# Sums over d in a three-layer interaction network: from Vector-engine reductions to ScalarE's accumulator

## The reference, cut to what matters

```python
B, M, D = 512, 32, 64            # SIZES = (128, 128, 128)
h = x0
for i in range(3):
    Wk = Ws[i].reshape(128, h.shape[1], M)
    xk = relu(einsum('bhd,bmd,ohm->bod', h, x0, Wk) + bs[i][None, :, None])
    if i != 2:
        outs.append(xk[:, :64]); h = xk[:, 64:]
    else:
        outs.append(xk)
return concatenate([o.sum(axis=-1) for o in outs], axis=1)     # (512, 256)
```

## Time and profile before

| | |
|---|---|
| median of 3 runs | 1762.95 us (1762.19 to 1766.04) |
| the profiled execution | 1765.33 us |
| its span, first to last instruction | 1763.5 us |
| mean granted TensorE clock | 0.993 |
| TensorE, Vector engine, ScalarE, GpSimd busy | 99%, 95%, 74%, 96% of the span |

### The profile page before, as it was taken

One profiled execution on the slowest core, in us unless ns is written; L12 is line 12 of the kernel. 1 busy time (PEld: TensorE's weight loads), 2 busy tenths in 40 slices (PEclk: granted clock), 3 DMA queues, 4 the chain that ended last, 5 costly groups with the idle time before them and its releaser, 6 DMA issues.

```text
span 1763.5 us, 19227 instructions
## 1 busy us (share of the span) xinstructions
PE 1742.0 (99%) x6740; PEld 1270.2 (72%) x6740; DVE 1676.0 (95%) x915; ACT 1307.9 (74%) x1218; POOL 1694.4 (96%) x451
## 2 busy tenths in 40 slices
PE   7899999999999999999999999999999999999998
PEld 4577777777777777777777777777777777777776
DVE  5999999999999999999999999999999999999996
ACT  3777777777777777777777777777777777777774
POOL 2799999999999999999999999999999999999996
PEclk8999999999999999999999999999999999999999
DMA  6424324334333243243243343332332432433410
GB/s 241 134 81 143 122 93 143 106 110 137 93 129 135 88 136 135 81 143 124 92 142 112 105 139 97 123 135 88 136 135 81 143 128 87 144 111 105 140 31 21
DMA packets 53600, 205.87 MB, mean 117 GB/s; under 512 B 10624, under 2 KB 11776, under 8 KB 45056
## 3 DMA queue, kind: packets, MB, share of 16 engines
q1 hardware_dynamic: 52992, 203.86, 35.0%
q10 hardware_dynamic: 512, 0.79, 0.2%
HBM read 153.75 MB, written 0.52 MB: 87 GB/s over the span
## 4 chain that ended last, share of the span: by engine, by line
PE 95%; DMA 2%; DVE 1%; ACT 1%; issue 0%; SPq 0%; POOL 0%; ACTq 0%; DVEq 0%; POOLq 0%
PE ACC L535 26%; PE ACC L526 26%; PE ACC L528 25%; PE ACC L519 15%; PE ACC L541 3%; DMA X<-in_xrows 1%; DMA H<-H 1%; DVE ZS L287 1%; DVE ZL L303 0%; POOL ZL L383 0%; ACT ZH L426 0%; ACT H L443 0%; ACT HP L409 0%; DVE S L317 0%; SPq L194 0%
## 5 line engine op out<-in xcount | busy, mean ns | idle before, releaser
L383 POOL TENSOR_TENSOR ZL<-ZS,ZH 128x2048 fp32r<-128x2048 f32 (+1 forms) x446 | 1693.7, 3846 | 60.9 <-ACT ZH L426 59.5
L287 DVE TENSOR_TENSOR ZS<-HP,X 128x2048 f32<-128x2048 f32 x448 | 1012.3, 2283 | 61.4 <-issue 46.4
L426 ACT ACTIVATE ZH<-ZS 128x2048 fp32r<-128x2048 f32 (+1 forms) x446 | 706.3, 1597 | 17.4 <-DVE ZS L287 15.5
L526 PE MATMUL ACC<-ZH,WL 128*128 128x512 f32 x1728 | 540.5, 427 | 5.1 <-DVE WL L261 4.2
L535 PE MATMUL ACC<-ZL,WH 128*128 128x512 f32 x1728 | 487.9, 396 | 7.0 <-DVE ZL L303 3.6
L528 PE MATMUL ACC<-ZH,WH 128*128 128x512 f32 x1728 | 486.7, 396 | 0.0
L409 ACT ACTIVATE HP<-H 128x512 f32<-128x512 f32 x256 | 152.8, 597 | 374.0 <-DVE ZS L287 361.9
L526 PEld LDWEIGHTS ACC<-ZH,WL 128*128 128x128 f32 x1728 | 326.0, 189 | 123.4 <-issue 51.6
L528 PEld LDWEIGHTS ACC<-ZH,WH 128*128 128x128 f32 x1728 | 325.1, 188 | 92.0 <-issue 15.3
L535 PEld LDWEIGHTS ACC<-ZL,WH 128*128 128x128 f32 x1728 | 324.4, 188 | 88.2 <-DVE ZL L303 5.2
L278 DVE TENSOR_TENSOR ZP<-HP,X 128x2048 f32<-128x2048 f32 x128 | 293.2, 2290 | 5.4 <-ACT HP L409 5.4
(11 more groups left out here) (34 smaller groups left out, 396.8 us busy)
## 6 DMA issues: line engine op xcount, KB each, us to landing
X<-in_xrows SPq DMA_DIRECT2D x62, 2048.0 KB, 7.6
H<-H SPq DMA_DIRECT2D x252, 128.0 KB, 2.3
XD<-in_xdup SPq DMA_DIRECT2D x64, 256.0 KB, 2.9
H<-H SPq DMA_DIRECT2D x252, 64.0 KB, 2.0
X<-in_xrows SPq DMA_DIRECT2D x4, 1024.0 KB, 7.9
X<-in_w SPq DMA_DIRECT2D x1, 896.0 KB, 10.5
X<-in_w SPq DMA_DIRECT2D x1, 832.0 KB, 14.8
H<-H ACTq DMA_DIRECT2D x4, 128.0 KB, 7.2
```

Source lines behind the costliest of these rows:

```text
L287: nc.vector.tensor_tensor(ZS[:, m % PSLOTS, :, :], h, x, ALU.mult).then_inc(product_ready, 1)
L383: nc.gpsimd.tensor_tensor(ZL[:, n % LSLOTS, c, :], ZS[:, m % PSLOTS, c, :], ZH[:, n % HSLOTS, c, :], ALU.subtract).then_inc(low_by_pool, 1)
L426: nc.scalar.activation(ZH[:, n % HSLOTS, c, :], src, ACT.Copy).then_inc(high_ready, 1)
L526: nc.tensor.matmul(acc, wl[:, k, :], ZH[:, n % HSLOTS, c, :], start=(first and k == 0), stop=False)
```

## The change

ScalarE's relu that fed a sum is cut into eight pieces of 64 columns, one for each sample of the tile. Each piece writes back into the accumulation bank that it reads and hands the sum of its outputs, one number per row, straight to its column of S12 or S3 (`accum_out`). `R12`, `R3`, the Vector engine's `sum12` and `sum3` and their semaphores are gone; a zeroed tile `BLANK` takes R3's place for the warm-up matmuls. The relus of the hidden rows (L443) are as they were. The last transposes wait for relu_done in place of the sums, and the last one also for out12_ready.

```diff
--- before.py
+++ after.py
@@ -118,8 +118,7 @@
         ZS = sb("ZS", [128, PSLOTS, G, T])
         ZH = sb("ZH", [128, HSLOTS, G, T], f32r)
         ZL = sb("ZL", [128, LSLOTS, G, T], f32r)
-        R12 = sb("R12", [128, T])
-        R3 = sb("R3", [128, T])
+        BLANK = sb("BLANK", [128, T])
         S12 = sb("S12", [128, B + BT])
         S3 = sb("S3", [128, B])
 
@@ -154,7 +153,6 @@
         low_by_pool, low_by_dve, low_used = sem("low_by_pool"), sem("low_by_dve"), sem("low_used")
         hidden_done = [sem("hidden_done2"), sem("hidden_done3")]
         relu_done = [sem(f"relu_done{n}") for n in range(3)]
-        sums12, sums3 = sem("sums12"), sem("sums3")
         tr_done, tr12_done = sem("tr_done"), sem("tr12_done")
         outs_ready, out12_ready, stored = sem("outs_ready"), sem("out12_ready"), sem("stored")
 
@@ -303,20 +301,6 @@
                 nc.vector.tensor_tensor(ZL[:, n % LSLOTS, :, :], ZP[:, :, :], ZH[:, n % HSLOTS, :, :],
                                         ALU.subtract).then_inc(low_by_dve, 1)
 
-            def sum12(i):
-                lo, hi = (0 if live(i) else HID), (2 * HID if live(i - 1) else HID)
-                if live(i):
-                    dve.wait_ge(relu_done[0], i + 1)
-                if live(i - 1):
-                    dve.wait_ge(relu_done[1], i)
-                nc.vector.reduce_sum(S12[lo:hi, BT * i:BT * i + BT],
-                                     R12[lo:hi, :].rearrange("p (b d) -> p b d", d=D), AX.X).then_inc(sums12, 1)
-
-            def sum3(t):
-                dve.wait_ge(relu_done[2], t + 1)
-                nc.vector.reduce_sum(S3[:, BT * t:BT * t + BT],
-                                     R3[:, :].rearrange("p (b d) -> p b d", d=D), AX.X).then_inc(sums3, 1)
-
             def gather12(n):
                 if n < BLOCKS - 1:
                     dve.wait_ge(tr_done, n + 1)
@@ -350,8 +334,6 @@
                     if i == 1:
                         low(i, 1, 0)
                     product(i, 1, 2)
-                if 0 <= i - 1 <= TILES:
-                    sum12(i - 1)
                 if live(i - 1):
                     if i > 1:
                         low(i, 1, 0)
@@ -360,20 +342,17 @@
                     product(i, 2, 0)
                     product(i, 2, 1)
                     product(i, 2, 2)
-                    if live(i - 3):
-                        sum3(i - 3)
                     low(i, 2, 0)
                     product(i, 2, 3)
             for n in range(BLOCKS - 1):
                 gather12(n)
                 gather3(n)
             gather12(BLOCKS - 1)
-            sum3(TILES - 1)
             gather3(BLOCKS - 1)
 
         @block.gpsimd
         def _(pool):
-            nc.gpsimd.memset(R3[:, :], 0.0).then_inc(blank, 1)
+            nc.gpsimd.memset(BLANK[:, :], 0.0).then_inc(blank, 1)
             for g in POOL_NO:
                 n, m = SPLIT_NO[g], SLOT_NO[g]
                 if n >= LSLOTS:
@@ -425,6 +404,14 @@
                     src = ZS[:, SLOT_NO[g] % PSLOTS, c, :]
                 nc.scalar.activation(ZH[:, n % HSLOTS, c, :], src, ACT.Copy).then_inc(high_ready, 1)
 
+            def relu_sums(acc, rows, b, to, t, done):
+
+                for n in range(BT):
+                    d = slice(D * n, D * n + D)
+                    last = nc.scalar.activation(acc[rows, d], acc[rows, d], ACT.Relu, bias=b[rows, :],
+                                                accum_out=to[rows, BT * t + n:BT * t + n + 1])
+                last.then_inc(done, 1)
+
             def relu(t, layer):
                 acc = ACC[LAYER_NO[t + layer, layer] % BANKS]
                 if layer == 0 and t < HEADS:
@@ -433,9 +420,7 @@
                     act.wait_ge(low_used, SPLIT_NO[t + layer, layer, Q - 1 if layer else 0] + 1)
                 b = bias_sb[:, layer:layer + 1]
                 if layer == 2:
-                    if t >= 1:
-                        act.wait_ge(sums3, t)
-                    nc.scalar.activation(R3[:, :], acc[:, :], ACT.Relu, bias=b).then_inc(relu_done[2], 1)
+                    relu_sums(acc, slice(0, 2 * HID), b, S3, t, relu_done[2])
                     return
                 hid, rest = (slice(HID, 2 * HID), slice(0, HID))[::1 if layer == 0 else -1]
                 if t >= 1:
@@ -444,10 +429,7 @@
                                      bias=b[hid, :]).then_inc(hidden_done[layer], 1)
                 if spread_by_act(t):
                     spread_hidden(act, t, layer)
-                if t + layer >= 1:
-                    act.wait_ge(sums12, t + layer)
-                nc.scalar.activation(R12[rest, :], acc[rest, :], ACT.Relu,
-                                     bias=b[rest, :]).then_inc(relu_done[layer], 1)
+                relu_sums(acc, rest, b, S12, t + layer, relu_done[layer])
 
             def high_w1():
                 act.wait_ge(w1_summed, 1)
@@ -578,7 +560,7 @@
             def keep_warm(acc, count):
 
                 for _ in range(count):
-                    nc.tensor.matmul(acc, R3[:, 0:OUT], R3[:, :], start=True, stop=True)
+                    nc.tensor.matmul(acc, BLANK[:, 0:OUT], BLANK[:, :], start=True, stop=True)
 
             pe.wait_ge(blank, 1)
             keep_warm(ACC[0][:, :], WARM)
@@ -598,14 +580,16 @@
                         if i == TILES + 1 and q == Q - 1:
                             pe.wait_ge(cleared, 2)
                             pe.wait_ge(ident_loaded, 16)
-                            pe.wait_ge(sums12, TILES + 1)
-                            pe.wait_ge(sums3, 128 * (BLOCKS - 1) // BT)
+                            pe.wait_ge(relu_done[0], TILES)
+                            pe.wait_ge(relu_done[1], TILES)
+                            pe.wait_ge(relu_done[2], 128 * (BLOCKS - 1) // BT)
                             for n in range(BLOCKS - 1):
                                 turn12(n)
                                 turn3(n)
                             turn12(BLOCKS - 1)
                         group(i, layer, q, acc)
-            pe.wait_ge(sums3, TILES)
+            pe.wait_ge(relu_done[2], TILES)
+            pe.wait_ge(out12_ready, 1)
             turn3(BLOCKS - 1)
```

## The result

The changed kernel takes 1848.49 us, the median of 4 runs (1848.01 to 1848.78), against 1762.65 us (1762.19 to 1766.04): ratio 1.0485, 95% interval 1.0473 to 1.0497, 86 us slower. The profiled execution took 1848.67 us with a span of 1846.9 us.

A forecast was written before the change was run, and what follows sets the result against it. TensorE bounds the kernel at 26.83 us a tile; ScalarE's period would become 28.41 us, so 1765.33 + 98 + 1 = 1864 us profiled, 1862 us as median; range 1761 to 2000 us.

The forecast's parts named there:

- What bounds it: TensorE, busy 100.00 of 100 us, sets the pace at 26.83 us a tile; saving Vector-engine time is worth nothing.
- The price of a piece: ScalarE's 64-column relu with its sum was taken as 0.31 us from start to start, bounded by 0.21 and 0.50.
- much slower: Rival: the sum is a ScalarE step of its own; 1996 us at 0.40 us a piece, 2145 at 0.50; chance 0.30.
- p: Cost of one 64-column piece on ScalarE from start to start, 24 pieces per tile; taken as 0.31 us.
- The forced wait: ScalarE idles 2.34 us per tile before the bank copy, behind a 6.52 us chain from high(i,2,0) through the Vector engine.
- The period: ScalarE's time per tile, 20.97 + 24p, is 28.41 us, 1.58 us more than now.
- The sum: 62 full passes at 1.58 us give +98 us, the tail +1 us; passes at both ends cost nothing, up to 3 us.
- The no-change rival: ScalarE's pieces overlap and the sum is free, p = 0.21 us; TensorE stays full, 1763 to 1764 us; chance 0.18.
- the threshold of 0.244: The piece cost in us at which ScalarE's period equals 26.83 us; from there the change costs time.
- TensorE's gaps: Rival: gaps of some 1.5 us per tile lower TensorE's clock, at most some +10 us; no chance of its own given.
- The bank: At (i,1,0) TensorE waits for the third layer's relu bank, about 3.3 us later; not a second cost.
- ScalarE's share: ScalarE's busy share was to be 93 to 95%, with one wait of about 2.3 us per tile left.

The follow-up runs named there:

- pieces_in_gap: The changed kernel with only the eight pieces of the first layer's relu moved behind high(i,2,1), into ScalarE's wait for the bank copy: 1767.37 us, ratio 1.0023.

## Why the prediction was right

The forecast was 1862 us and slower; 1848.5 us came. By its steps:

- **What bounds it.** That TensorE hides all that the Vector engine saves: shown, by the run without sums (ratio 0.9985).
- **The price of a piece.** Taken 0.31 us, measured 0.29, and the reasons for it were wrong. The relu alone is 0.21 us from start to start, so the neighbours do overlap. The earlier trace rows spoke for that more than I read from them: of the three relus that fed a sum two overlapped with their follower (914.86 and 921.98, each 0.59 us to the next start), where the prediction counted one place of two. Nor is a sum out before the next piece starts: the fetch at 901.35 lasts until 901.54, the next piece starts at 901.44. The fetch is a step of its own, which I kept for the "much slower" rival, but only 0.08 us of it shows, since it overlaps on both sides and its 199 ns row is mostly covered. Two errors of about the same size, 0.10 too much for the relu and 0.08 too little for the fetch, cancelled: that p came out near 0.31 is luck. What was not luck is that the ends worked out from rows (0.21 and 0.50) held it.
- **The forced wait.** Forecast 2.34 us a tile, measured 2.36; chain 6.52 us, measured 6.57. This is the term that decided the sign: without it ScalarE's work, 18.63 + 6.96 = 25.6 us, fits into 26.83. The run that only moved eight pieces into it took the loss back.
- **The period.** Forecast 20.97 + 24p = 28.41; with p = 0.29 it gives 27.93, measured 28.15. The 0.2 us left is in gaps around the pieces: the three sets take 2.57 + 2.32 + 2.42 = 7.31 us and not 24 x 0.29 = 6.96, while the rest of ScalarE's tile, 25.80 - 7.31 = 18.49 us, is a little shorter than the 18.63 forecast. (25.80 us is from the end of the wait at 888.45 to 914.25, where the next one begins.)
- **The sum.** 62 x (28.15 - 26.83) = 82 us, against 98 forecast; measured 86 with the ends, for which the prediction had 1 us and up to 3 more. Of the 0.26 us a tile too much, 0.13 are the pieces (7.44 against 7.31) and 0.14 the rest of ScalarE's work; the wait was 0.02 us too short.
- **The no-change rival and the page's figure.** The page "ScalarE: Activation LUTs" of the Trainium skill, section "What ACT_TABLE_LOAD costs", led to 0.240 us a piece for an activation alone; the run without the sum has 0.21 us, and the fetch is what that figure leaves out. At 0.240 us a piece the change would have stayed 0.004 us under the threshold of 0.244, and cost nothing.
- **The much slower rival** had the mechanism (a fetch of its own) and not the price.
- **TensorE's gaps.** The wait at (i,1,0) was forecast as 1.5 us and the share as 94 to 95%; measured 1.07 us and 95% of the span, 96% in the steady part. The clock stayed at 1.00 in the steady part; among the experiments the fall was seen only with longer gaps.
- **The bank.** I said that TensorE's wait for the bank is where the period shows and not a second cost. The runs bear that out: the wait goes in pieces_in_gap without touching that bank.
- **ScalarE's share** was forecast as 93 to 95%. That contradicted my own sum (1 - 2.34 / 28.41 = 92%); it is 91% in the steady part.

What the prediction missed is that the chain has a second forced wait, at copy_operand(i,2,1), which only the pieces of the third layer hide.

## What to carry to other kernels

An engine's idle time is not all room. Before moving work to an engine that looks 25% idle, follow each of its waits back: a wait at the end of a chain that this same engine starts is there however late it runs, and only work placed inside it is free. Place moved work there first; the same 24 pieces cost 86 us in one order and 4 us in another. And freeing an engine beside the bound is worth nothing until the freed time is filled with something that shortens the bound.

## What the runs showed of the hardware

- A relu of 64 columns with bias follows the last one after 0.21 us; with `accum_out` a READ_ACCUMULATOR row of 0.20 us stands behind it and the pitch becomes 0.29 us. Into SBUF, from SBUF, the pitch was 0.33 us.
- A Vector-engine subtraction with both inputs in SBUF, 128x512, lasted 3.69 us in the mean and up to 11.18 us beside a busy GpSimd, and 128x1024 only 1.21 us where GpSimd was idle when it started, 1.69 where GpSimd was about to pause.
- TensorE's clock stayed at its upper level over waits of 1.07 us in each tile and was at the lower one behind waits of 3.83 and 4.28 us (and of 1.96 us near the end of the kernel before).
